# Slot stage of a hard-routed feed-forward: matmul order, a third buffer for turned one-hots, wider loads and stores

## The chip, the cores and the metric

The kernel is one launch on one core of a Trainium2 chip. The metric is the device time of that launch in microseconds. The kernel before took 5747.51 us, the median of three runs (5745.52 to 5748.87).

## The reference

The program computes, on x of shape (16, 256, 128) in float32:

1. causal attention with 16 heads of 8, added to x and normalised;
2. a "fast feed-forward" block: x is standardised to xn; q, k and v each come from a hard-routed feed-forward of xn; attention over 256 tokens; then y + fff(y) with a fourth one, f; added and normalised;
3. a gated causal scan;
4. six layers of local attention (16 heads of 64, window 32) and gated feed-forward; added and normalised.

The change is in part 2. One hard-routed feed-forward (D = 128, LW = 16, DEPTH = 8, 255 nodes, 256 leaves) is

```python
node = zeros
for _ in range(8):
    logit = einsum('bsd,bsd->bs', x, nw[node]) + nb[node]
    node = 2 * node + 1 + (logit > 0)
leaf = node - 255
h = act(einsum('bsd,bsdl->bsl', x, w1[leaf]) + b1[leaf])
out = einsum('bsl,bsld->bsd', h, w2[leaf]) + b2[leaf]
```

so each of the 4096 tokens goes down a tree to a leaf of its own and through that leaf's 128x16 and 16x128 matrices.

## The kernel before

Five engines run in order, each its own stream of instructions, and wait for each other by semaphores: PE (matmul), ACT, DVE, POOL and SP (which issues plain DMAs). routed_feed_forwards (L686) runs twice: for q, k and v together (modules m = 0, 1, 2), and later for f alone. In it:

**Routing.** All node logits of a token are one matmul (L855), the leaf's one-hot comes from a second (L862). Eight leaves form a chunk, so 32 chunks of 128 hidden columns. Counting the tokens by chunk gives each token a position: its chunk's tokens fill whole slots of 128 rows, 64 slots in all (positions, L1110, on DVE). A token's row holds its 128 values and 32 bf16 one-hot values of its leaf within the chunk: ROW = 144 words. POOL writes the rows to DRAM (leaf_rows) with 32 indirect DMAs per module (scatter), and reads the results back from leaf_out with 32 more (gather), in the order scatter 0, 1, 2, gather 0, 1, 2.

**Slots.** Four slots are a group, q; a module has 16 groups. SP loads a group (L812) into one of three xrow buffers, with 128 partitions x 4 pieces of 576 bytes. Then:

- PE turn(q), L889: four fp32 transposes into px (L896) and four bf16 matmuls that turn the one-hots into pl (L898);
- ACT turned(q), L997: copies px to xT (two buffers) and pl to ohT (two buffers). The second copy waits for out_done of group q-2, as that group's output matmuls read the same ohT buffer;
- DVE first_weights(q), L1155: reads each slot's chunk number into a register and copies that chunk's first weights to W1 (L1171) and its bias rows to B_slot (L1173);
- PE hidden(q), L909: per slot, an fp32 matmul (L918, two passes in hardware) and a bf16 matmul that adds bias and a mask of the other leaves (L919); ACT takes the activation to hm (L1010);
- PE second(q), L922: per slot, an fp32 matmul with the second weights (L929, two passes) and a bf16 one for the bias (L930); ACT copies py to yrow (L1016, two buffers); SP stores it to leaf_out (L820).

The order on PE is turn(i), hidden(i-1), second(i-2), then four register loads of chunk numbers for group i (chunks_of); turn(i+1) waits until both copies of turned(i) are done. ACT's order is turned(i), hidden(i-1), outputs(i-2). The last module's routing (m = 2) is laid between the steps i = 0 to 15, a part in each step; k's and f's routing runs ahead of the slots. SP goes through load(i), then store(i-5). The weights of a module are 4 MB, loaded by load_weights in four DMAs; v's take q's place after q's last store.

Of the kernel before, what the change touches and what calls it, by code (L numbers as in the profile page):

```python
# [8 lines left out]
BF16 = mybir.dt.bfloat16  # L9
F32R = mybir.dt.float32r  # L10
U32 = mybir.dt.uint32
# [7 lines left out]
D = 128  # L19
# [567 lines left out]
CHUNKS = 32  # L587
# [8 lines left out]
SRING = 3  # L596

# [88 lines left out]
def routed_feed_forwards(nc, dram, src, modules, act_func, rows_dram, out_dram, scattered, gathered, bias_dram, KV):  # L686
# [6 lines left out]
    with ExitStack() as ctx:  # L693
# [3 lines left out]
        def sb(name, shape, dt=F32):  # L697
# [14 lines left out]
        one_row = sb("one_row", [128, 1])  # L712
        spare = modules[0][1][:].rearrange("p t d -> p (t d)")
        bias_rows = spare[:, 0:512 * n_mod].rearrange("p (m n) -> p m n", n=512)
        bias_rest = spare[:, 512 * n_mod:1024 * n_mod].rearrange("p (m n) -> p m n", n=512)
        late = KV[:].rearrange("p a t d -> p (a t d)")
        nodes = spare[:, 1024 * n_mod:(1024 + LEAVES) * n_mod].rearrange("p (m n) -> p m n", n=LEAVES)
        bias_parts = late[:, 0:n_mod * PIECES * 256].bitcast(BF16).rearrange("p (m c n) -> p m c n", c=PIECES, n=512)
        bits = sb("bits", [128, 2, 2, GT], BF16)
        onehot = sb("onehot", [128, 2, 2, GT], BF16)  # L720
        oc = sb("oc", [128, 2, CHUNKS, NT], BF16)
        mod8 = sb("mod8", [128, 2, NT, BROWS], BF16)
        place = sb("place", [128, CHUNKS, NT])
# [5 lines left out]
        pos_f = sb("pos_f", [128, NT])  # L729
        pos = sb("pos", [128, n_mod, NT], U32)  # L730
# [4 lines left out]
        W = sb("W", [128, CHUNKS, 256])  # L735
# [4 lines left out]
        xrow = sb("xrow", [128, SRING, SG, ROW])  # L740
        xT = sb("xT", [128, 2, SG * 128])
        ohT = sb("ohT", [BROWS, 2, SG * 128], BF16)
        hm = sb("hm", [128, 2, SG * 128])
        yrow = sb("yrow", [128, 2, SG * 128])
# [9 lines left out]
            oc_done oc_ready cnt_done before_ready place_ready count_ready small restart_set tiles_ready chunk_ready pos_ready mod_ready  # L754
# [18 lines left out]
        @block.sync  # L773
        def _(sp):
            for dst, name in consts:
                sp.dma_start(dst[:], dram[name]).then_inc(s["consts_in"], 16)
            for m, (name, _) in enumerate(modules):
                sp.dma_start(nodes[:, m], dram[name + "_nw"]).then_inc(s["nodes_in"], 16)
                sp.dma_start(node_b[:, m], dram[name + "_nb"]).then_inc(s["nodes_in"], 16)
            for m, (name, _) in enumerate(modules):  # L780
                sp.dma_start(bias_rows[:, m, :].rearrange("p (h n) -> p h n", h=2), dram[name + "_b"].rearrange("(h p) n -> p h n", h=2))\
                    .then_inc(s["bias_in"], 16)
            def load_weights(m):

# [20 lines left out]
            def load(q):  # L805
                m, G = divmod(q, SGROUPS)
                r = q % SRING
                if q >= SRING:
                    sp.wait_ge(s["xt_done"], q - SRING + 1)
                if G == 0:  # L810
                    sp.wait_ge(scattered[m], 16 * NT)
                sp.dma_start(xrow[:, r], rows_dram[m % 2][128 * SG * G:128 * SG * (G + 1)].rearrange("(j p) c -> p j c", p=128))\  # L812
                    .then_inc(s[f"in{r}"], 16)

            def store(q):
                m, G = divmod(q, SGROUPS)
                sp.wait_ge(s["y_ready"], q + 1)
                if G == 0 and m >= 2:
                    sp.wait_ge(gathered[m - 2], 16 * NT)
                sp.dma_start(out_dram[m % 2][128 * SG * G:128 * SG * (G + 1)].rearrange("(j p) c -> p j c", p=128),  # L820
                             yrow[:, q % 2].rearrange("p (j c) -> p j c", j=SG)).then_inc(s[f"y_out{q % 2}"], 16)
                if G == SGROUPS - 1 and m + 2 < n_mod:
                    load_weights(m + 2)

            for i in range(n_steps + SRING + 2):
                if i < n_steps:
                    load(i)
                if i >= SRING + 2:
                    store(i - SRING - 2)

        @block.tensor
        def _(pe):
# [56 lines left out]
            def turn(q):  # L889
                r = q % SRING  # L890
                pe.wait_ge(s[f"in{r}"], 16 * (q // SRING + 1))
                if q >= 1:
                    pe.wait_ge(s["xt_ready"], q)
                    pe.wait_ge(s["oh_ready"], q)
                for j in range(SG):
                    nc.tensor.transpose(px[:, 128 * j:128 * j + 128], xrow[:, r, j, 0:D], ident[:])  # L896
                for j in range(SG):
                    mm = nc.tensor.matmul(pl[0:BROWS, 128 * j:128 * j + 128], xrow[:, r, j, D:ROW].bitcast(BF16), ident_b[:],  # L898
                                          start=True, stop=True)
                mm.then_inc(s["xt_done"], 1)  # L900
# [20 lines left out]

            def second(q, chunks):  # L922
# [3 lines left out]
                for j in range(SG):  # L926
                    cols = slice(128 * j, 128 * j + 128)
                    w = weights[q // SGROUPS][:, bass.ds(chunks[j], 1), 128:256].rearrange("p o n -> p (o n)")
                    nc.tensor.matmul(py[:, cols], hm[:, q % 2, cols], w, start=True, stop=False)  # L929
                    mm = nc.tensor.matmul(py[:, cols], ohT[:, q % 2, cols], B_slot[:, q % 3, j, 128:256],  # L930
                                          start=False, stop=True)
# [46 lines left out]
        def _(act):  # L978
# [18 lines left out]
            def turned(q):  # L997
# [14 lines left out]
            def outputs(q):  # L1012
                act.wait_ge(s["out_done"], q + 1)
                if q >= 2:
                    act.wait_ge(s[f"y_out{q % 2}"], 16 * (q // 2))
                nc.scalar.activation(yrow[:, q % 2, :], py[:], ACT.Copy).then_inc(s["y_ready"], 1)  # L1016
# [22 lines left out]
        def _(pool):  # L1039
# [32 lines left out]
            def gather(m):  # L1072
                for half in range(2):
                    pool.wait_ge(s[f"y_out{half}"], 16 * SGROUPS // 2 * (m + 1))
# [14 lines left out]
        def _(dve):  # L1089
# [20 lines left out]
            def positions(m):  # L1110
# [21 lines left out]
                nc.vector.scalar_tensor_tensor(place[:], tiles_at[:].unsqueeze(2).to_broadcast([128, CHUNKS, NT]), 128.0, place[:],  # L1132
                                               ALU.mult, ALU.add).then_inc(s["tiles_ready"], 1)
                dve.wait_ge(s["tiles_ready"], 3 * m + 1)
                nc.vector.tensor_tensor(place[:], place[:], oc[:, m % 2], ALU.mult).then_inc(s["tiles_ready"], 1)
                dve.wait_ge(s["tiles_ready"], 3 * m + 2)
                nc.vector.tensor_reduce(pos_f[:], place[:].rearrange("p c t -> p t c"), AX_X, ALU.add).then_inc(s["tiles_ready"], 1)
                dve.wait_ge(s["tiles_ready"], 3 * m + 3)
                nc.vector.tensor_copy(pos[:, m, :], pos_f[:]).then_inc(s["pos_ready"], 1)
# [357 lines left out]
def layouts_b(i):  # L1497

    out = {}
    for m in "qkvf":  # L1500
# [10 lines left out]
        out[m + "_w"] = w.reshape(CHUNKS, D, 256)  # L1511
# [1186 lines left out]
```

## Time and profile before

| | us |
|---|---|
| median of three runs | 5747.51 |
| profiled execution, whole | 5710.15 |
| its span, first to last instruction | 5708.4 |
| causal attention, up to | 883 |
| q, k, v: routing and slots | 883 to 1606 |
| last gather, attention over tokens | 1606 to 1720 |
| f: routing, scatter, slots, gather | 1720 to 2034 |
| residual, norm, scan | 2034 to 2270 |
| six layers of local attention | 2270 to 5708 |

The profile is of one execution. Times in rows are microseconds from the start of its span. PE is matmul, PEld PE's weight load (it overlaps PE). PEclk is the share of full speed that the clock throttle grants to PE. "[idle before <-releaser]" at the end of a row says how long the engine was idle ahead of it and who ended that. A row with x2 or x4 merges that many instructions.

### The profile page before, as it was taken

Reading aid. Unit: us, or ns where it says so; the run is one execution under the profiler, and the core shown is the slowest. Engines: PE = TensorE matmul, PEld = TensorE weight load, DVE = VectorE, ACT = ScalarE, POOL = GpSimd, SP = SyncE. Lnnn points to the kernel's source line nnn. Section 1 sums busy time; section 2 is a strip of 40 time slices with the busy share of each in tenths; the row PEclk is TensorE's granted clock in tenths of the full one; section 3 lists DMA queues with packets and bytes.
Section 4 is the critical chain, followed back from the end, with each engine's and each line's share of the span. In section 5 each row is a group of like instructions: output and inputs, shape, how many; then the busy total and the mean of one; then the engine's idle time right before and its main releaser. Section 6 shows DMA issues by size and latency. Waiting matters only on the chain. (4 is left out here: it accounts for less than half of the span.)

```text
span 5708.4 us, 191262 instructions
## 1 busy us (share of the span) xinstructions
PE 4628.9 (81%) x74176; PEld 3577.0 (63%) x74192; DVE 3909.8 (68%) x6605; ACT 3409.6 (60%) x6019; POOL 2762.6 (48%) x3241
## 2 busy tenths in 40 slices
PE   7888855659754824799999989998999899989993
PEld 3444422435432513688778877887788788878881
DVE  4666644321123136799889988998899889989983
ACT  3554411112121104689779977997898789878981
POOL 2222203240222011677667766776677577767750
PEclk8888857765566556899999999999999999999995
DMA  2000003132202100211111111111111111121110
GB/s 93 1 0 0 0 0 112 57 94 56 59 25 78 48 11 16 56 47 45 53 51 46 45 49 50 45 46 54 50 45 46 55 44 47 44 59 45 46 41 15
DMA packets 214059, 253.21 MB, mean 44 GB/s; under 512 B 34996, under 2 KB 139700, under 8 KB 211636
## 3 DMA queue, kind: packets, MB, share of 16 engines
q1 hardware_dynamic: 205524, 230.77, 14.4%
q0 software_dynamic: 8192, 17.84, 1.0%
q8 instruction: 218, 3.57, 0.3%
q14 instruction: 125, 1.02, 0.1%
HBM read 70.76 MB, written 39.32 MB: 19 GB/s over the span
## 5 line engine op out<-in xcount | busy, mean ns | idle before, releaser
L2398 POOL TENSOR_TENSOR d_rc<-d_rc,d_rs 128x512 f32<-128x512 f32 x768 | 964.4, 1277 | 537.9 <-DVE d_rs L2481 523.6
L2408 POOL TENSOR_TENSOR d_rc<-d_rc,d_inv 128x1024 f32<-128x1024 f32 x384 | 722.9, 1903 | 161.1 <-DVE d_inv L2502 159.3
L1964 PE MATMUL d_pair<-d_W_high,d_xs_high 128*128 128x512 f32 x1152 | 525.8, 456 | 106.4 <-DVE d_W_low L2467 40.7
L2481 DVE TENSOR_TENSOR d_rc<-d_pair,d_rot 128x512 f32<-128x512 f32 x768 | 528.3, 688 | 102.5 <-ACT d_sq L2213 81.7
L2481 DVE TENSOR_TENSOR d_rs<-d_pair,d_rot 128x512 f32<-128x512 f32 x768 | 523.5, 682 | 0.0
L2213 ACT ACTIVATE d_sq<-d_pair 128x512 f32<-128x512 f32 x768 | 435.9, 597 | 126.8 <-PE d_pair L1964 112.1
L1964 PE MATMUL d_pair<-d_W_high,d_xs_low 128*128 128x512 f32 x1152 | 465.1, 404 | 5.7 <-issue 5.7
L1964 PE MATMUL d_pair<-d_W_low,d_xs_high 128*128 128x512 f32 x1152 | 464.6, 403 | 0.0
L2491 DVE TENSOR_REDUCE d_ss<-d_sq 128x16 f32<-128x1024 f32 x384 | 448.6, 1211 | 0.0
L2111 PE MATMUL d_pair<-d_OT,d_Wo 128*128 128x128 f32 x3072 | 380.4, 278 | 0.0
L2008 PE MATMUL d_pair<-d_ident,d_rc 128*128 128x128 f32 x3072 | 367.6, 273 | 1.0 <-ACT d_sq L2213 1.0
L2111 PEld LDWEIGHTS d_pair<-d_OT,d_Wo 128*128 128x128 f32 x3072 | 364.6, 195 | 0.1
L2008 PEld LDWEIGHTS d_pair<-d_ident,d_rc 128*128 128x128 f32 x3072 | 342.8, 141 | 2.1 <-issue 1.7
L1964 PEld LDWEIGHTS d_pair<-d_W_high,d_xs_high 128*128 128x128 f32 x1152 | 221.3, 192 | 187.3 <-issue 89.3
L2050 PEld LDWEIGHTS d_pair<-d_KT,d_QT 64*32 64x32 f32 x24576 | 256.1, 105 | 129.4 <-issue 129.4
L2083 PE MATMUL d_pair<-d_VW,d_PT 64*32 64x64 f32 x18432 | 300.5, 228 | 44.5 <-issue 44.3
L2509 DVE TENSOR_REDUCE d_mx<-d_pair 128x16 f32<-128x1024 f32 x192 | 234.8, 1223 | 142.5 <-PE d_pair L2050 142.4
L2050 PE MATMUL d_pair<-d_KT,d_QT 64*32 64x64 f32 x24576 | 291.2, 226 | 44.4 <-issue 44.3
L2083 PEld LDWEIGHTS d_pair<-d_VW,d_PT 64*32 64x32 f32 x18432 | 258.4, 106 | 108.6 <-issue 108.6
L2083 PE MATMUL d_pair<-d_V,d_PT 64*32 64x64 f32 x6144 | 300.0, 229 | 14.4 <-issue 14.4
L2262 ACT ACTIVATE d_V<-d_pair 128x512 f32<-128x512 f32 x384 | 227.9, 594 | 139.7 <-PE d_pair L2083 100.4
L312 ACT ACTIVATE a_first<-a_bank,a_late_bias,a_later 128x256 bf16<-128x256 f32 x256 | 128.9, 565 | 282.3 <-PE a_bank L162 282.1
(348 smaller groups left out, 11836.6 us busy)
## 6 DMA issues: line engine op xcount, KB each, us to landing
d_VW<-d_V SPq DMA_DIRECT2D x768, 128.0 KB, 2.4
d_VW<-d_V SPq DMA_DIRECT2D x576, 64.0 KB, 2.0
q_xrow<-leaf_rows SPq DMA_DIRECT2D x48, 288.0 KB
leaf_out<-q_yrow SPq DMA_DIRECT2D x48, 256.0 KB
d_W_whole<-Wqkv_dram SPq DMA_DIRECT2D x7, 1536.0 KB, 7.5
leaf_rows<-a_zeros SPq DMA_DIRECT2D x8, 1152.0 KB, 11.8
f_xrow<-leaf_rows SPq DMA_DIRECT2D x16, 288.0 KB, 3.2
q_W<-q_w_dram SPq DMA_DIRECT2D x4, 1024.0 KB, 10.2
```

The lines of the kernel that those rows point to most:

```text
L1964: mm = nc.tensor.matmul(target, x_part[:, t.par, :], w_part[:, c, :], start=n == 0, stop=n == 2)
L2008: mm = nc.tensor.transpose(ps[:, hp // 4, (hp % 4) * 128:(hp % 4) * 128 + 128], source(hp), ident[:])
L2050: mm = nc.tensor.matmul(s_pair[WIN * w:WIN * w + WIN, odd, hp * DH:hp * DH + DH], QT[rows, hp, WIN * w:WIN * w + WIN], KT[rows, hp, at + W ...
L2083: mm = nc.tensor.matmul(o_pair[WIN * w:WIN * w + WIN, odd, hp * DH:hp * DH + DH], PT[rows, hp, WIN * w:WIN * w + WIN], window_values(t, w, ...
L2111: mm = nc.tensor.matmul(proj_bank[:, 0:128], Wo[:, hp, :], OT[:, hp, :], start=hp == 0, stop=hp == HP - 1)
L2213: nc.scalar.activation(sq[:, half, 512 * j:512 * j + 512], ps[:, j, :], ACT.Square).then_inc(s[f"s{qk}{j}_ready"], 1)
L2262: nc.scalar.activation(V[:, t.par, j, :], v_pair[:, j, :], ACT.Copy).then_inc(s[f"v{j}_ready"], 1)
L2398: nc.gpsimd.tensor_tensor(own[:, :, a, :], own[:, :, a, :], other[:, :, 1 - a, :], ALU.add).then_inc(s[f"add{qk}_ready"], 1)
L2408: nc.gpsimd.tensor_tensor(heads(rc[:, t.par, half, :]), heads(rc[:, t.par, half, :]), inv[:, t.par, half, :].unsqueeze(2).to_broadcast([12 ...
L2481: ins = nc.vector.tensor_tensor(heads(target), heads(ps[:, j, :]), rot[:, t.par, half, cs, :].unsqueeze(1).to_broadcast([128, HP, DH]), AL ...
L2491: nc.vector.tensor_reduce(ss[:, half, :], heads(sq[:, half, :]), AX_X, ALU.add).then_inc(s[f"ss{qk}_ready"], 1)
L2509: nc.vector.tensor_reduce(mx[:], s_pair[:].rearrange("p a (h n) -> p (a h) n", n=DH), AX_X, ALU.max)\
```

## The change

- hidden and second issue the four fp32 matmuls of a group first and the four bf16 ones after them. The whole group is one accumulation: start at its first matmul, stop at its last.
- ohT has three buffers; turned(q) waits for the output matmuls of group q-3.
- SP loads and stores two groups at once (WIDE = 8 slots). In DRAM a block of 1024 rows is now laid out with 8 consecutive rows per partition, so each partition moves one piece. So that a token still comes to its slot, positions gets five integer operations that reorder the bits of a row number.
- The weights in DRAM are laid out by partition first, so a partition's part of a load is one piece. load_weights(0) is issued after the bias parts are stored, since the bias staging now lies in W.
- bits, onehot and place lie in q's output tensor, which makes room; so POOL's first gather waits until the last chunk numbers are made.

```diff
+WIDE = 2 * SG
...
+        place = spare[:, 1024:2048].rearrange("p (c t) -> p c t", t=NT)
+        bits = spare[:, 2048:3072].bitcast(BF16).rearrange("p (b j t) -> p b j t", j=2, t=GT)
+        onehot = spare[:, 3072:4096].bitcast(BF16).rearrange("p (b j t) -> p b j t", j=2, t=GT)
...
-        xrow = sb("xrow", [128, SRING, SG, ROW])
+        xrow = sb("xrow", [128, SRING, WIDE, ROW])
-        ohT = sb("ohT", [BROWS, 2, SG * 128], BF16)
+        ohT = sb("ohT", [BROWS, 3, SG * 128], BF16)
-        yrow = sb("yrow", [128, 2, SG * 128])
+        yrow = sb("yrow", [128, 2, WIDE * 128])
...
-                    sp.dma_start(weights[m][:, chunks, :], dram[name + "_w"][chunks].rearrange("c p n -> p c n")).then_inc(s[f"w_in{m}"], 16)
-            load_weights(0)
+                    sp.dma_start(weights[m][:, chunks, :], dram[name + "_w"][:, chunks, :]).then_inc(s[f"w_in{m}"], 16)
...
             sp.wait_ge(s["bias_out"], 16 * 2 * PIECES * n_mod)
+            load_weights(0)
...
+            def load(k):
+                m, first = divmod(k, SGROUPS // 2)
+                if k >= SRING:
+                    sp.wait_ge(s["xt_done"], 2 * (k - SRING) + 2)
+                if first == 0:
+                    sp.wait_ge(scattered[m], 16 * NT)
+                sp.dma_start(xrow[:, k % SRING], rows_dram[m % 2][128 * WIDE * first:128 * WIDE * (first + 1)].rearrange("(p j) c -> p j c", j=WIDE))\
+                    .then_inc(s[f"in{k % SRING}"], 16)
...
+            for k in range(n_steps // 2 + SRING + 1):
+                if k < n_steps // 2:
+                    load(k)
+                if k >= SRING + 1:
+                    store(k - SRING - 1)
...
-                    nc.tensor.matmul(ph[:, q % 2, cols], W1[:, q % 2, j, :], xT[:, q % 2, cols], start=True, stop=False)
-                    mm = nc.tensor.matmul(ph[:, q % 2, cols], B_slot[:, q % 3, j, 0:128], ohT[:, q % 2, cols], start=False, stop=True)
+                    nc.tensor.matmul(ph[:, q % 2, cols], W1[:, q % 2, j, :], xT[:, q % 2, cols], start=j == 0, stop=False,
+                                     skip_group_check=True)
+                for j in range(SG):
+                    cols = slice(128 * j, 128 * j + 128)
+                    mm = nc.tensor.matmul(ph[:, q % 2, cols], B_slot[:, q % 3, j, 0:128], ohT[:, q % 3, cols], start=False, stop=j == SG - 1,
+                                          skip_group_check=True)
...
-                if q >= 2:
-                    act.wait_ge(s["out_done"], q - 1)
-                nc.scalar.activation(ohT[:, q % 2, :], pl[0:BROWS, :], ACT.Copy).then_inc(s["oh_ready"], 1)
+                if q >= 3:
+                    act.wait_ge(s["out_done"], q - 2)
+                nc.scalar.activation(ohT[:, q % 3, :], pl[0:BROWS, :], ACT.Copy).then_inc(s["oh_ready"], 1)
...
             def gather(m):
+                if m == 0:
+                    pool.wait_ge(s["chunk_ready"], n_mod)
...
-                nc.vector.tensor_copy(pos[:, m, :], pos_f[:]).then_inc(s["pos_ready"], 1)
+                nc.vector.tensor_copy(pos_i[:], pos_f[:]).then_inc(s["row_ready"], 1)
+                dve.wait_ge(s["row_ready"], 5 * m + 1)
+                nc.vector.tensor_scalar(pos_slot[:], pos_i[:], 7, WIDE - 1, ALU.logical_shift_right, ALU.bitwise_and).then_inc(s["row_ready"], 1)
+                nc.vector.tensor_scalar(pos_row[:], pos_i[:], 127, 3, ALU.bitwise_and, ALU.logical_shift_left).then_inc(s["row_ready"], 1)
+                nc.vector.tensor_scalar(pos_i[:], pos_i[:], 0xFFFFFC00, None, ALU.bitwise_and).then_inc(s["row_ready"], 1)
...
+                nc.vector.tensor_tensor(pos_row[:], pos_row[:], pos_slot[:], ALU.bitwise_or).then_inc(s["row_ready"], 1)
...
+                nc.vector.tensor_tensor(pos[:, m, :], pos_row[:], pos_i[:], ALU.bitwise_or).then_inc(s["pos_ready"], 1)
```

second changes as hidden does, store as load does.

## Rows read from the trace of the kernel before

**Rows 1.** The page: granted TensorE clock in 40 slices, in tenths.

```profile
PEclk8888857765566556899999999999999999999995
```

**Rows 2.** Busy time by stage: us, busy (instructions) of PE, PEld, DVE, ACT, POOL; PEclk; DMA share; GB/s.

```profile
1210.00:1286.00 76.00, 13.47 (x47) 8.38 (x46) 2.10 (x8) 2.68 (x6) 50.34 (x53) 0.50 0.34 112
1286.00:1436.00 150.00, 138.31 (x486) 88.49 (x487) 27.15 (x123) 33.13 (x63) 5.67 (x6) 0.50 0.21 59
...
1474.00:1606.00 132.00, 121.15 (x420) 77.34 (x420) 21.23 (x96) 28.33 (x54) 0.00 (x0) 0.50 0.18 49
...
1820.00:1981.00 161.00, 146.44 (x512) 93.53 (x512) 19.63 (x112) 35.77 (x65) 0.00 (x0) 0.50 0.19 53
```

**Rows 3.** Order of time, one step, low clock: start, us, engine, line, instruction, idle before.

```profile
1385.33 1.09 PE L896 MATMUL q_ps_x<-q_ident,q_xrow 128*128 128x128 f32 x4 [0.77 <-ACT q_ohT L1004]
1386.35 0.61 PE L898 MATMUL q_ps_leaf<-q_ident_b,q_xrow 128*32 128x128 bf16 x4
...
1386.89 0.80 PE L918 MATMUL q_ps_hid<-q_xT,q_W 128*128 128x128 f32 x2
...
1387.83 0.80 PE L918 MATMUL q_ps_hid<-q_xT,q_W 128*128 128x128 f32 x2
...
1395.24 1.09 PE L896 MATMUL q_ps_x<-q_ident,q_xrow 128*128 128x128 f32 x4 [0.77 <-ACT q_ohT L1004]
```

**Rows 4.** Waits, 1300 to 1430 us: us in total, times, longest.

```profile
ACT q_ohT L1004 <- PE q_ps_y L930: 90.0, 13, 6.9
```

**Rows 5.** Order of time, steps under routing, high clock.

```profile
1117.01 0.49 PE L918 MATMUL q_ps_hid<-q_xT,q_W 128*128 128x128 f32 x2
...
1117.59 0.49 PE L929 MATMUL q_ps_y<-q_W,q_hm 128*128 x2
...
1120.73 0.63 PE L896 MATMUL q_ps_x<-q_ident,q_xrow 128*128 128x128 f32 x4 [0.77 <-ACT q_ohT L1004]
...
1121.61 0.55 PEld L862 LDWEIGHTS q_ps_route<-q_bits,q_paths 128*128 128x128 bf16 x4
...
1154.87 0.63 PE L896 MATMUL q_ps_x<-q_ident,q_xrow 128*128 128x128 f32 x4 [0.77 <-ACT q_ohT L1004]
```

**Rows 6.** The page's groups: busy, mean ns of one, idle before.

```profile
L2111 PE MATMUL d_pair<-d_OT,d_Wo 128*128 128x128 f32 x3072 | 380.4, 278 | 0.0
```

**Rows 7.** Busy time and clock in short stretches.

```profile
889.00:892.50 3.50, 3.50 (x18) 2.90 (x17) 0.00 (x0) 2.09 (x4) 0.00 (x0) 0.50 0.69 159
892.50:896.00 3.50, 2.59 (x16) 1.77 (x16) 0.00 (x0) 2.47 (x5) 0.00 (x0) 0.95 0.95 298
...
1110.00:1111.00 1.00, 0.25 (x3) 0.28 (x4) 0.17 (x2) 0.98 (x3) 0.00 (x0) 1.00 0.00 0
...
1112.00:1113.00 1.00, 1.00 (x2) 0.48 (x3) 0.39 (x3) 0.55 (x1) 0.00 (x0) 0.50 0.53 161
```

**Rows 8.** Order of time: DVE, positions and first weights.

```profile
937.40 0.18 DVE L1139 CAST q_pos<-q_pos_f 128x32 uint32<-128x32 f32 x1
...
1111.69 0.23 DVE L1171 COPY q_W<-q_W 128x128 f32 x1 [0.52 <-issue]
...
1112.56 0.23 DVE L1171 COPY q_W<-q_W 128x128 f32 x1 [0.52 <-issue]
...
1113.64 0.23 DVE L1171 COPY q_W<-q_W 128x128 f32 x1 [0.73 <-issue]
```

**Rows 9.** f's stage: instructions of f_W, and order of time.

```profile
L1171 DVE COPY f_W<-f_W x64: 226/227/442, 1779.9 to 1960.8; 128x128 f32 x64
...
1741.52 0.34 SPq L801 DMA_DIRECT2D f_B<-leaf_bias_f  x1
...
1815.63 0.96 POOL L1069 DMA_INDIRECT leaf_rows<-f_rows,f_pos  x1 [0.30 <-issue]
...
1980.33 0.60 ACT L1016 ACTIVATE f_yrow<-f_ps_y 128x512 f32<-128x512 f32 x1 [4.12 <-PE f_ps_y L930]
1983.88 0.97 POOL L1076 DMA_INDIRECT b_Q<-leaf_out,f_pos  x1 [167.29 <-DMA leaf_out<-f_yrow]
```

More of the change, by code:

```diff
@@ L729, in routed_feed_forwards @@
         pos_f = sb("pos_f", [128, NT])
+        pos_i = sb("pos_i", [128, NT], U32)
+        pos_row = sb("pos_row", [128, NT], U32)
+        pos_slot = sb("pos_slot", [128, NT], U32)
         pos = sb("pos", [128, n_mod, NT], U32)
@@ L753, in routed_feed_forwards @@
         names = """consts_in nodes_in memset_done rows_done rows_ready bits_done bits_ready match_done onehot_ready
-            oc_done oc_ready cnt_done before_ready place_ready count_ready small restart_set tiles_ready chunk_ready pos_ready mod_ready
+            oc_done oc_ready cnt_done before_ready place_ready count_ready row_ready small restart_set tiles_ready chunk_ready pos_ready mod_ready
             in0 in1 in2 w_in0 w_in1 w_in2 bias_in bias_split bias_out b_in mask_in w1_ready b_ready xt_done xt_ready oh_ready hid_done hm_ready out_done y_ready y_out0 y_out1""".split()
@@ L803, in _ @@
                 load_weights(1)
[L805 to L810, printed above, removed]
-                    sp.wait_ge(scattered[m], 16 * NT)
[L812 to L818, printed above, removed]
+            def load(k):
[3 more added lines that the diff above has]
+                if first == 0:
+                    sp.wait_ge(scattered[m], 16 * NT)
+                sp.dma_start(xrow[:, k % SRING], rows_dram[m % 2][128 * WIDE * first:128 * WIDE * (first + 1)].rearrange("(p j) c -> p j c", j=WIDE))\
+                    .then_inc(s[f"in{k % SRING}"], 16)
@@ L819, in store @@
+            def store(k):
+                m, first = divmod(k, SGROUPS // 2)
+                sp.wait_ge(s["y_ready"], 2 * k + 2)
+                if first == 0 and m >= 2:
                     sp.wait_ge(gathered[m - 2], 16 * NT)
-                sp.dma_start(out_dram[m % 2][128 * SG * G:128 * SG * (G + 1)].rearrange("(j p) c -> p j c", p=128),
-                             yrow[:, q % 2].rearrange("p (j c) -> p j c", j=SG)).then_inc(s[f"y_out{q % 2}"], 16)
-                if G == SGROUPS - 1 and m + 2 < n_mod:
+                sp.dma_start(out_dram[m % 2][128 * WIDE * first:128 * WIDE * (first + 1)].rearrange("(p j) c -> p j c", j=WIDE),
+                             yrow[:, k % 2].rearrange("p (j c) -> p j c", j=WIDE)).then_inc(s[f"y_out{k % 2}"], 16)
+                if first == SGROUPS // 2 - 1 and m + 2 < n_mod:
@@ L823, in store @@
                     load_weights(m + 2)
[L825 to L829, printed above, removed]
+            for k in range(n_steps // 2 + SRING + 1):
[3 more added lines that the diff above has]
+                    store(k - SRING - 1)
         @block.tensor
@@ L889, in turn @@
             def turn(q):
-                r = q % SRING
-                pe.wait_ge(s[f"in{r}"], 16 * (q // SRING + 1))
+                r, at = q // 2 % SRING, SG * (q % 2)
+                pe.wait_ge(s[f"in{r}"], 16 * (q // 2 // SRING + 1))
                 if q >= 1:
@@ L895, in turn @@
                 for j in range(SG):
-                    nc.tensor.transpose(px[:, 128 * j:128 * j + 128], xrow[:, r, j, 0:D], ident[:])
+                    nc.tensor.transpose(px[:, 128 * j:128 * j + 128], xrow[:, r, at + j, 0:D], ident[:])
                 for j in range(SG):
-                    mm = nc.tensor.matmul(pl[0:BROWS, 128 * j:128 * j + 128], xrow[:, r, j, D:ROW].bitcast(BF16), ident_b[:],
+                    mm = nc.tensor.matmul(pl[0:BROWS, 128 * j:128 * j + 128], xrow[:, r, at + j, D:ROW].bitcast(BF16), ident_b[:],
                                           start=True, stop=True)
@@ L928, in second @@
                     w = weights[q // SGROUPS][:, bass.ds(chunks[j], 1), 128:256].rearrange("p o n -> p (o n)")
-                    nc.tensor.matmul(py[:, cols], hm[:, q % 2, cols], w, start=True, stop=False)
-                    mm = nc.tensor.matmul(py[:, cols], ohT[:, q % 2, cols], B_slot[:, q % 3, j, 128:256],
-                                          start=False, stop=True)
+                    nc.tensor.matmul(py[:, cols], hm[:, q % 2, cols], w, start=j == 0, stop=False, skip_group_check=True)
+                for j in range(SG):
+                    cols = slice(128 * j, 128 * j + 128)
+                    mm = nc.tensor.matmul(py[:, cols], ohT[:, q % 3, cols], B_slot[:, q % 3, j, 128:256], start=False, stop=j == SG - 1,
+                                          skip_group_check=True)
                 mm.then_inc(s["out_done"], 1)
@@ L1013, in outputs @@
                 act.wait_ge(s["out_done"], q + 1)
-                if q >= 2:
-                    act.wait_ge(s[f"y_out{q % 2}"], 16 * (q // 2))
-                nc.scalar.activation(yrow[:, q % 2, :], py[:], ACT.Copy).then_inc(s["y_ready"], 1)
+                k, odd = divmod(q, 2)
+                if k >= 2 and odd == 0:
+                    act.wait_ge(s[f"y_out{k % 2}"], 16 * (k // 2))
+                nc.scalar.activation(yrow[:, k % 2, 512 * odd:512 * odd + 512], py[:], ACT.Copy).then_inc(s["y_ready"], 1)
             for k in range(NG):
@@ L1072, in gather @@
             def gather(m):
+                if m == 0:
+                    pool.wait_ge(s["chunk_ready"], n_mod)
                 for half in range(2):
-                    pool.wait_ge(s[f"y_out{half}"], 16 * SGROUPS // 2 * (m + 1))
+                    pool.wait_ge(s[f"y_out{half}"], 16 * SGROUPS // 4 * (m + 1))
                 for t in range(NT):
@@ L1131, in positions @@
                 dve.wait_ge(s["place_ready"], 2 * m + 2)
[L1132 removed]
+                nc.vector.scalar_tensor_tensor(place, tiles_at[:].unsqueeze(2).to_broadcast([128, CHUNKS, NT]), 128.0, place,
                                                ALU.mult, ALU.add).then_inc(s["tiles_ready"], 1)
                 dve.wait_ge(s["tiles_ready"], 3 * m + 1)
[L1135 removed]
+                nc.vector.tensor_tensor(place, place, oc[:, m % 2], ALU.mult).then_inc(s["tiles_ready"], 1)
                 dve.wait_ge(s["tiles_ready"], 3 * m + 2)
[L1137 removed]
+                nc.vector.tensor_reduce(pos_f[:], place.rearrange("p c t -> p t c"), AX_X, ALU.add).then_inc(s["tiles_ready"], 1)
                 dve.wait_ge(s["tiles_ready"], 3 * m + 3)
[L1139 removed]
+                nc.vector.tensor_copy(pos_i[:], pos_f[:]).then_inc(s["row_ready"], 1)
[3 more added lines that the diff above has]
+                nc.vector.tensor_scalar(pos_i[:], pos_i[:], 0xFFFFFC00, None, ALU.bitwise_and).then_inc(s["row_ready"], 1)
+                dve.wait_ge(s["row_ready"], 5 * m + 4)
+                nc.vector.tensor_tensor(pos_row[:], pos_row[:], pos_slot[:], ALU.bitwise_or).then_inc(s["row_ready"], 1)
+                dve.wait_ge(s["row_ready"], 5 * m + 5)
+                nc.vector.tensor_tensor(pos[:, m, :], pos_row[:], pos_i[:], ALU.bitwise_or).then_inc(s["pos_ready"], 1)
                 if m >= 1:
@@ L1510, in layouts_b @@
         w[:, :, 1] = a("w2").reshape(CHUNKS, 128, D)
-        out[m + "_w"] = w.reshape(CHUNKS, D, 256)
+        out[m + "_w"] = w.reshape(CHUNKS, D, 256).transpose(1, 0, 2)
         b = np.zeros((CHUNKS, CHUNK_LEAVES, 2, 128), np.float32)
```

14 lines of the change are left out of this document (6 added, 8 removed).

## The prediction

> **What bounds the kernel now.** I read the summary first, then the busy time by stage, then the waits and the order of instructions inside one step of the slot stage, because that is what the edit touches. The summary shows a TensorE clock at 5 tenths in several of its slices, from the seventh to the sixteenth [rows 1]. [...] Two stretches are of another kind: from 1210 to 1286 us, and from 1436 to 1474, POOL issues its indirect transfers and PE hardly runs (13.47 us of the first 76); what PE's work costs there hardly matters.
>
> I call a group of four slots a step. One step at the low clock takes 9.91 us, first transpose to first transpose (1385.33 to 1395.24) [rows 3]. In it PE turns the rows (1.56 us to the first hidden matmul, 1386.89), does four hidden and four output pairs at 0.94 us (1386.89 to 1387.83), 7.52 us, and then waits: the rest, 9.91 - 1.56 - 7.52 = 0.83 us, is ACT's copy to ohT, which starts after PE's last output matmul and holds PE's next transposes (0.77 us of PE idle on that row). Over 130 us ACT's ohT copy waits 90.0 us for PE, 13 times [rows 4]. DVE waits for PE too. So the bound is PE, plus one stall per step.
>
> **The change part by part.** *The third ohT buffer.* The copy waited for the output matmuls of two steps back, which stand at the end of the current step. With three buffers it waits for those of three steps back, long done, so it runs right after the turning. Gone: 0.83 us a step. What PE waits for next is due earlier: ACT's hidden copy has half a step, and the y copy of the step before is due only before the output matmuls.
>
> *Matmuls apart.* A pair of two fp32 passes and one bf16 matmul takes 0.94 us at the low clock (1386.89 to 1387.83) and 0.57 at the high one (1117.01 to 1117.59) [rows 3, 5]. In an unbroken run of fp32 passes of the same 128x128x128 shape each costs 380.4 us / 3072 = 0.124 us, at a clock that is mostly high [rows 6]. So of 0.57 us some 0.23 are the two passes (the mean holds some low clock), and 0.05 the bf16 matmul, half a pass (at the low clock four leaf matmuls, bf16 too, took 0.54 us with their switch, 1386.35 to 1386.89, and four fp32 transposes 1.02 [rows 3]); about 0.29 is the alternation, one switch there and back. At the low clock the same split is 0.43 + 0.11 + 0.40. Eight pairs a step are now two runs, so six of eight alternations go: 6 x 0.40 = 2.4 us at the low clock, 6 x 0.29 = 1.75 at the high one. Bounds: nothing, if the gap belongs to each fp32 pair whatever follows (then the row of 0.124 us could not be), and 8 x 0.40 = 3.2 us. I take six. [...]
>
> At an unchanged clock a step is then 9.91 - 0.83 - 2.4 = 6.7 us.
>
> *The clock.* This is the largest term, and indirect. At the high clock it fell right after the stall: PE idle at 1110 us (busy 0.25 of 1 us), clock still 1.00, and 0.50 at 1112 [rows 7]; it was back at the high level by 1117, where a pair takes 0.57 us [rows 5], after four route matmuls of 512 columns without a pause. In the plain steps, where a switch gap follows every two passes, it never rises [rows 2]. After the change the switch gaps and the stall, 0.83 + 8 x 0.40 = 4.0 us of a low-clock step, shrink to some 0.8, with no pause over 0.3 us. That is far nearer to the route stretch than to the plain step, so I expect the rise within about two steps, and then it should hold: the stall that preceded each fall is gone. [...]
>
> At the high clock a step is 0.88 (turning, 1120.73 to the next weight load at 1121.61) + 2 x (4 x 0.575 - 3 x 0.29 = 1.43) = 3.74 us on PE [rows 5]. DVE becomes a near tie: four slots at 0.87 us (1111.69 to 1112.56) are 3.5 us [rows 8]. ACT's four copies are shorter (4 x 0.6 us, the copy at 1980.33 [rows 9]). I take 3.85 us; 3.6 and 4.6 are the ends (DVE's slow pace, 1.08 us from 1112.56 to 1113.64, four times and 0.3 for its start).
>
> *Loads and stores in pairs of groups.* Half as many on SP, one run of 4608 or 4096 bytes per partition instead of pieces of 576 or 512. They hide behind PE: three buffers are six groups now, and the load is issued five steps ahead. Only the ends show: POOL's gather began at 1983.88, 3.55 us after the start of the last copy at 1980.33, for the store between them [rows 9]; the first load is alike. A transfer twice as large there costs 0 to 1.5 us at each end; 0.75 x 4 = 3 us.
>
> *Row numbers.* Five more small DVE instructions after the cast of the positions (0.18 us [rows 8]), about 0.2 us each, ahead of the scatter: 1 us for each of q, k, f (v's lie under the slots); bounds 0 and 2 us each. 3 us.
>
> *Edits at nothing.* load_weights(0) moves on SP past the bias stores and delays the bias reads queued behind it. In f the bias reads were issued at 1741.52 and DVE's first W1 copy came at 1779.9 [rows 9]: 38 us of cover. The aliased tiles add one wait, of POOL's first gather for the last chunk numbers, which precede it anyway, since POOL scatters v first. Without that cover the bias reads would cost the weights' transfer ahead of them: 4 MB at the 298 GB/s of 892.5 to 896 us [rows 7] is 14 us, each in q and f.
>
> **The sum,** against the profiled execution (span 5708.4, whole 5710.15 us). Steps under routing (1065 to 1175 us): two took 17.07 us ((1154.87 - 1120.73) / 2 [rows 5]); they lose two stalls (1.6), twelve alternations (3.5) and the low stretch between 1111 and 1115 us (half of 3.4, 1.7), which leaves 10.3; with DVE at 8 x 0.87 = 7.0 us and four routing operations on top I take 10.7: 6.4 pairs of steps x 6.4 us = 41 us. Plain steps of q: (150 + 132) / 9.91 = 28.5, times 6.06 = 172 us, less two climbs of two steps at 6.7 us (2 x 5.7 = 11): 161. f: 161 / 9.91 = 16.2, times 6.06 = 98, less one climb: 93. The stretches under POOL's transfers: 0. Added: 6. Together 41 + 161 + 93 - 6 = 289 us, 5421 for the profiled execution. The median of the runs shown is 37 us above it; that difference I carry unchanged: 5747.5 - 289 = 5458 us.
>
> **The rivals.**
> *The clock stays low in plain steps.* For it: they run at 0.50 throughout now. Against: [rows 7]. Then 44.7 steps x 3.2 = 144, + 41 - 6 = 179 us: 5568. [...]
> *DVE becomes the bound,* at 4.6 us a step: 44.7 x 5.3 = 237, - 17 + 41 - 6 = 255 us: 5493. For it: the slow pace in [rows 8]. Against: that pace is rare.
> *The edit doesn't do what it says:* the gap belongs to the fp32 pair. Then the stall alone goes, and the clock stays: 44.7 x 0.83 + 6.4 x 1.6 - 6 = 41 us: 5706. [...] Against: [rows 6].
> *Slower:* neighbouring tokens of a chunk now lie eight rows apart, and POOL's indirect transfers may slow. They go at 0.96 + 0.30 = 1.26 us [rows 9]; of eight series of 32, seven are on the path, 224 transfers. Above 2.55 us each the gain is used up; at 3.0 us it is 5459 + 224 x 1.74 = 5849. Against: the pace is POOL's own, the bytes are the same, and tokens were scattered over the chunks before.
>
> **How the numbers follow.** Forecast 0.66, clock stays low 0.15, DVE 0.10, no effect of the grouping 0.05, slower 0.03, an even outcome 0.01. The forecast's own range is 5410 to 5510 (step 3.6 to 4.6 us; up to 30 us of luck in how far PE gets under POOL's transfers). The range of 5405 to 5570 takes in the low clock and leaves out 0.15 or so. Measurements of this kernel tell 0.2% (11 us) from no change: faster 0.95, same 0.02, slower 0.03.
>
> **What would show it.** In the profile after: PE's wait for ohT gone; runs of eight fp32 passes with one gap behind; granted clock near 1.0 in f's slot work and its span near 68 us instead of 161; plain steps of 3.7 to 4.1 us; the gaps under POOL's transfers as long as before. A clock of 0.5 there with steps of 6.7 us means the first rival; steps near 5 with PE waiting for DVE's W1 copy the second.

## The result

The changed kernel takes 5494.61 us (median of 4 runs, 5490.34 to 5499.0), the kernel before 5748.19 (4 runs): ratio 0.956, interval 0.954 to 0.958. The gain is 254 us; 290 were forecast (5458). The profiled execution took 5493.6 us, its span is 5491.8.

The granted clock by slices, and the busy time by stage, in the columns of [rows 2]:

```profile
PEclk8877776687687569999999999999999999999995
```
```profile
1110.00:1176.00 66.00, 55.06 (x430) 39.94 (x433) 29.29 (x106) 28.95 (x55) 0.00 (x0) 1.00 0.24 86
...
1300.00:1356.00 56.00, 45.85 (x379) 36.66 (x377) 21.00 (x95) 26.66 (x48) 0.00 (x0) 0.98 0.34 121
1404.00:1452.00 48.00, 39.23 (x316) 31.57 (x315) 17.16 (x78) 22.59 (x40) 0.00 (x0) 0.95 0.25 93
1684.00:1746.00 62.00, 50.73 (x427) 40.57 (x426) 18.29 (x104) 31.31 (x56) 0.00 (x0) 0.99 0.29 100
```
The slot work that stood at 0.50 in [rows 2] now runs at 0.95 to 1.00, and f's slots, from the first turned group to the start of the gather, take 82 us instead of 163. To the start of the last copy of outputs it is 78 us (1678.90 to 1756.86), where 68 were forecast for the stretch that took 161 before. And PE is busy only 82 of 100 us there, where it was busy 92: part of what was saved on PE has become idle time of PE. One step of f, PE alone, then what PE waited for between 1686 and 1742 us (the wait, then us in total, times, longest):

```profile
1704.46 0.63 PE L900 MATMUL f_ps_x<-f_ident,f_xrow 128*128 128x128 f32 x4 [0.99 <-issue]
...
1705.02 0.40 PE L902 MATMUL f_ps_leaf<-f_ident_b,f_xrow 128*32 128x128 bf16 x4
...
1705.35 1.16 PE L922 MATMUL f_ps_hid<-f_xT,f_W 128*128 128x128 f32 x8
...
1706.44 0.39 PE L926 MATMUL f_ps_hid<-f_ohT,f_B_slot 32*128 32x128 bf16 x4
...
1706.76 1.16 PE L937 MATMUL f_ps_y<-f_W,f_hm 128*128 x8
...
1707.85 0.39 PE L940 MATMUL f_ps_y<-f_B_slot,f_ohT 32*128 32x128 bf16 x4
...
1709.13 0.63 PE L900 MATMUL f_ps_x<-f_ident,f_xrow 128*128 128x128 f32 x4 [0.89 <-issue]
```
```profile
PE f_ps_x L900 <- issue: 10.2, 11, 1.0
```
The two blocks of matmuls are as forecast: 1705.35 to 1706.76 is 1.41 us (1.43 in the prediction). The step is not: 4.67 us here, 4.70 on average, against 3.85. The missing 0.85 us is one pause, 0.89 us ahead of the next transposes, and "issue" says that no semaphore held it. What PE's sequencer (it runs ahead of the matmuls: the first read behind them in PE's stream begins at 1706.46, and they end at 1708.24) did in it stands in the view of line L911, the reads of chunk numbers (kind, times, ns, first and last start):

```profile
L911 PEldq TENSOR_LOAD <-f_chunk_no x4: 296/298/305, 1706.5 to 1708.4; - x4
L911 PEldq FUSED_REGOPS  x4: 146/148/151, 1706.8 to 1708.7; - x4
L911 PEldq SEQ_ASSERT  x4: 18/18/18, 1707.0 to 1708.9; - x4
```
Each of the four reads takes 0.64 us to the start of the next. They begin at 1706.46, behind the step's last matmul in the sequencer's order, and end at 1708.96, while the queued matmuls run out at 1708.24 (1707.85 + 0.39). So the stall on ohT of [rows 3] is gone, and a pause of about the same length for the reads stands in its place.

Where the time went, by the starts of the stages in the two traces (us):

| | before | changed | less |
|---|---|---|---|
| attention and norm, unchanged code, up to the first transpose of part 2 | 888.4 | 922.2 | -33.8 |
| q, k, v: routing up to the first turned group | 118.8 | 120.2 | -1.4 |
| first 16 steps (with v's routing between them) | 178.2 | 146.0 | 32.2 |
| the other 32, to the start of the last gather | 424.0 | 277.4 | 146.6 |
| last gather and attention over tokens | 115.5 | 115.8 | -0.3 |
| f: routing up to the first turned group | 96.0 | 97.3 | -1.3 |
| f: slots, to the start of the gather | 163.0 | 82.0 | 81.0 |
| f's gather to the end, unchanged code | 3724.5 | 3730.9 | -6.4 |
| span | 5708.4 | 5491.8 | 216.6 |

The changed part gives 256.8 us. The unchanged attention is 33.8 us longer in this trace, because the profiled execution of before had a higher clock there:

```profile
300.00:500.00 200.00, 172.24 (x1204) 88.70 (x1204) 135.28 (x213) 91.74 (x165) 42.85 (x44) 0.86 0.00 0
```
```profile
300.00:500.00 200.00, 176.01 (x1192) 90.00 (x1191) 121.05 (x190) 91.93 (x164) 44.41 (x44) 0.80 0.00 0
```
The same code ran at a granted clock of 0.86 in the one (the first row, before) and 0.80 in the other. These 33.8 us are most of the 37 by which the profiled execution of before lay below its median.

### The profile page after: what moved, and what is told of

Read it like the earlier page. It is cut to its first block and busy times, and to the rows that moved or that the text cites. A ratio compares the mean times of both kernels' runs of the same rounds, so it can differ in the third digit from the quotient of the medians.

```text
span 5491.8 us, 191188 instructions
## 1 busy us (share of the span) xinstructions
PE 4393.8 (80%) x74176; PEld 3461.5 (63%) x74192; DVE 3912.9 (71%) x6625; ACT 3422.4 (62%) x6019; POOL 2766.2 (50%) x3241
```

## The experiments

They ran on two other chips (e1 to e8 on one, e9 to e11 on the other), on which the kernel before takes 5590 to 5599 us, and each ratio is to the kernel before on the same chip; what differs is told at e5 and e6. Beside each ratio to the kernel before stand two lengths read from the profile as in the table above: q's (first transposes to the start of the last gather) and f's.

| | median us | ratio (95%) | q | f | plain step |
|---|---|---|---|---|---|
| e5 kernel before | 5592.3 | | 472.1 | 163.0 | 9.91 |
| e1 third buffer | 5535.1 | 0.989 (0.985 to 0.994) | 426.1 | 151.6 | 9.11 |
| e2 grouping | 5320.8 | 0.953 (0.949 to 0.956) | 275.1 | 86.2 | 4.66 to 4.94 |
| e7 third buffer, half the grouping | 5317.0 | 0.951 (0.949 to 0.954) | 288.0 | 89.1 | 7.89, then 4.70 |
| e3 third buffer and grouping | 5314.9 | 0.952 (0.948 to 0.955) | 273.9 | 81.6 | 4.70 |
| e6 changed kernel | 5319.4 | 0.950 (0.948 to 0.952) | 278.7 | 81.9 | 4.70 |
| e4 changed kernel, reads spread | 5276.1 | 0.944 (0.940 to 0.947) | 244.7 | 70.5 | 3.74 to 4.78 |
| e11 the same again | 5284.6 | 0.944 (0.942 to 0.946) | 244.9 | 73.2 | 3.74 to 4.63 |
| e8 the same, no bounds at the read | 5285.7 | 0.944 (0.942 to 0.946) | 249.0 | 73.5 | 3.74 to 4.93 |
| e10 e3 with reads spread | 5271.3 | 0.941 (0.940 to 0.943) | 241.3 | 72.0 | 3.74 to 4.76 |
| e9 e2 with reads spread | 5326.2 | 0.951 (0.949 to 0.953) | 282.9 | 88.1 | 5.1 |

**e1: the third buffer alone.**

```diff
-        ohT = sb("ohT", [BROWS, 2, SG * 128], BF16)
+        ohT = sb("ohT", [BROWS, 3, SG * 128], BF16)
...
-                if q >= 2:
-                    act.wait_ge(s["out_done"], q - 1)
+                if q >= 3:
+                    act.wait_ge(s["out_done"], q - 2)
```

> The kernel before with a third ohT buffer and nothing else. Two theories of what it is worth. (A) At the low clock PE's wait is really for ohT, since its four chunk-number reads (4 x 0.64 us on PE's sequencer) finish while the queued matmuls still run: a plain step falls from 9.91 to about 9.1 us, 44.7 steps x 0.8 = 36 us, and the steps at the high clock gain nothing, because there the reads end as late as the copy does: about 5712 us, ratio 0.994. (B) The reads take the stall's place at the low clock too: 5748 us, ratio 1.000. (C) Removing the stall alone lets the clock rise in the plain steps: over 100 us gained, below 5650 us.

5535 us: the plain step is 9.11 us, as (A) has it. The reads are out of the way there because at the low clock (0.50) the queued matmuls last longer: a pair takes 0.94 us, against 0.57 at the high one [rows 3, 5]. In a step of e5, the kernel before, the reads end at 1264.0, 3 us before the transposes that ohT holds:

```profile
L907 PEldq SEQ_ASSERT  x4: 18/18/18, 1262.0 to 1264.0; - x4
...
1266.99 1.09 PE L896 MATMUL q_ps_x<-q_ident,q_xrow 128*128 128x128 f32 x4 [0.77 <-ACT q_ohT L1004]
```
The ratio is 0.989 where (A) had 0.994. What (A) had wrong is the steps under routing: a pair of them takes 13.84 us in e1's trace, not 17.07. Both members lost 0.8 us, and the low stretch that followed each stall went too. The busy time in two steps under routing, and then in plain steps of the same trace (columns of [rows 2]):

```profile
1087.50:1101.30 13.80, 13.80 (x82) 8.84 (x80) 5.53 (x20) 5.35 (x10) 0.00 (x0) 1.00 0.30 83
...
1198.00:1343.00 145.00, 145.00 (x511) 92.88 (x509) 29.88 (x128) 35.56 (x63) 52.04 (x56) 0.50 0.32 87
```
PE is busy all of the time in both, the first at the high clock and the second at the low one for 145 us on end. So PE's busy share does not tell the two levels apart. It also counts the switches between fp32 and bf16: in the plain steps they are 8 x 0.41 = 3.3 of the 9.11 us.

**e2 and e3: grouping alone, and with the third buffer.** The grouping is the diff of hidden and second.

> The kernel before with the fp32 and the bf16 matmuls of a group apart and nothing else; ohT keeps two buffers, loads and stores as before. (A) The grouping carries nearly the whole gain: the switches go, the clock rises in spite of the ohT copy's stall, and at the high clock PE's chunk-number reads would hold the next transposes as long as the copy does: steps of about 4.7 us, 5490 to 5505 us, ratio 0.956. (B) The stall of each step keeps the clock down: steps of 9.91 - 2.4 = 7.5 us, 44.7 x 2.4 + 20 = 127 us gained, about 5620 us, ratio 0.978.

> The kernel before with both: third ohT buffer and grouped matmuls, but loads, stores, row numbers and weights' layout as before. (A) The wide loads and stores are off the path and the five extra DVE operations cost 1 us each: 5490 us, within 6 us of the changed kernel, ratio 0.955. (B) The wide transfers carry part of the gain (fewer and longer pieces leave the DMA engines to others): 5510 us or more.

Both (A). The grouping alone brings the clock up in spite of the stall (from 1200 to 1240 us, in plain steps of q, it is 1.00, with 7.7 us of waits for ohT), and leaves 0 to 6 us to the third buffer (5320.8 against 5314.9 us, with ratios whose intervals overlap). In the steps under routing too e2 keeps the stall on ohT, and the clock stays at the high level; the busy time and the wait from there:

```profile
1060.00:1110.00 50.00, 42.23 (x330) 30.26 (x328) 21.82 (x80) 19.52 (x40) 0.00 (x0) 1.00 0.33 92
```
```profile
PE q_ps_x L896 <- ACT q_ohT L1010: 7.8, 8, 1.0
```
In e3 two steps of q still run at 0.50 (1148 to 1161 us), and show the grouped step at that level:

```profile
1147.68 1.11 PE L896 MATMUL q_ps_x<-q_ident,q_xrow 128*128 128x128 f32 x4
1148.73 0.61 PE L898 MATMUL q_ps_leaf<-q_ident_b,q_xrow 128*32 128x128 bf16 x4
1149.27 2.08 PE L918 MATMUL q_ps_hid<-q_xT,q_W 128*128 128x128 f32 x8
1151.28 0.60 PE L922 MATMUL q_ps_hid<-q_ohT,q_B_slot 32*128 32x128 bf16 x4
1151.81 2.08 PE L933 MATMUL q_ps_y<-b_KV,q_hm 128*128 x8
1153.82 0.60 PE L936 MATMUL q_ps_y<-q_B_slot,q_ohT 32*128 32x128 bf16 x4
1154.35 0.90 PE L896 MATMUL q_ps_x<-q_ident,q_xrow 128*128 128x128 f32 x3
```
This is 6.67 us, against 9.11 with the third buffer alone: 2.44 us, six switches of 0.41, as the prediction had it (2.4 us, and 6.7 for the step). From there the clock takes the step to 4.70 (0.96 from 1161 to 1175 us, 1.00 from 1200 to 1260).

**e4: where the reads stand.** The same four reads of chunk numbers, laid between the blocks of matmuls (shortened from the edit, the comments say where each stands):

```diff
+                chunk_of(i, 0)      # after turn(i)
+                chunk_of(q + 1, 1)  # in hidden, between fp32 and bf16
+                chunk_of(i, 2)      # after hidden
+                chunk_of(q + 2, 3)  # in second, between fp32 and bf16
-                if i < n_steps:
-                    chunks[i] = chunks_of(i)
```

> The changed kernel with PE's four chunk-number reads of a step no longer in a row at its end, but one after the turning, one between the fp32 and the bf16 matmuls of hidden, one after hidden and one between those of second. (A) If these reads (4 x 0.64 us on the sequencer, of which 0.9 to 1.0 us is not covered by queued matmuls) are what holds a step at 4.70 us, the pause of 0.9 us shrinks to a few tenths, and the step to about 3.9 us, where DVE's four slots (4 x 0.87 + 0.4) are next: some 55 steps x 0.8 = 44 us, about 5450 us, ratio to the kernel before 0.948. (B) If DVE or ACT sets the step, nothing moves: 5495 us, ratio 0.956, and PE's idle time stands elsewhere in the step.

(A). A step of f:

```profile
1496.53 0.65 PE L900 MATMUL f_ps_x<-f_ident,f_xrow 128*128 128x128 f32 x4
1497.12 0.40 PE L902 MATMUL f_ps_leaf<-f_ident_b,f_xrow 128*32 128x128 bf16 x4
1497.44 1.16 PE L931 MATMUL f_ps_hid<-f_xT,f_W 128*128 128x128 f32 x8
1498.54 0.39 PE L936 MATMUL f_ps_hid<-f_ohT,f_B_slot 32*128 32x128 bf16 x4
1498.86 1.16 PE L947 MATMUL f_ps_y<-f_W,f_hm 128*128 x8
1499.95 0.39 PE L951 MATMUL f_ps_y<-f_B_slot,f_ohT 32*128 32x128 bf16 x4
1500.27 0.66 PE L900 MATMUL f_ps_x<-f_ident,f_xrow 128*128 128x128 f32 x4
```
3.74 us without a pause: each read now runs while queued matmuls do. DVE's work per slot is unchanged, so DVE did not set the 4.70 us. Between steps of 3.74 us lie others of up to 4.78. No run tests what sets these, but the trace shows where PE pauses in them. In f from 1489 to 1536 us PE is busy 45.91 of 47, and waits only ahead of second's fp32 block, behind the third read. Most reads take PE's sequencer 0.30 us ahead of their check, some up to 0.74, and the longest one (0.742 us, from 1505.53) stands ahead of the longest pause. Busy time, PE's wait, the reads, and that pause:

```profile
1489.00:1536.00 47.00, 45.91 (x391) 36.66 (x388) 16.76 (x96) 27.84 (x50) 0.00 (x0) 1.00 0.33 117
```
```profile
PE f_ps_y L947 <- issue: 1.0, 3, 0.4
```
```profile
L920 PEldq TENSOR_LOAD <-f_chunk_no x48: 294/302/742, 1489.4 to 1535.3; - x48
```
```profile
1506.83 1.16 PE L947 MATMUL f_ps_y<-f_W,f_hm 128*128 x8 [0.41 <-issue]
```
The step of 4.78 us in q has a read of 0.99 us in the same place. Why a read is slow is not shown. In q, from 1170 to 1250 us, DVE waits for PE only 0.8 us of 80 and PE's sequencer waits up to 0.54 us at hidden for DVE's copies, so DVE is close behind.

**e5 and e6: the two kernels themselves on the chip of e1 to e4.**

> The kernel before itself, once more, for a profile on the chip on which the following runs are made: the runs with third buffer and grouping came from a chip on which it took 5590 us instead of 5748. (A) The difference lies where POOL issues its indirect transfers: there PE's steps take 30 to 54 us on the one and 10 us on the other, and the plain steps take 9.9 us on both. (B) It lies everywhere, as a clock or a slower memory would have it.

> The changed kernel itself, for comparison with third buffer plus grouping alone. (A) Wide loads, row numbers and layouts are worth nothing: its q stage and f stage, from first transposes to last gather, are as long as those of third_group within 5 us on the same kind of chip. (B) They are worth 10 us or more one way, most likely where POOL's transfers run, as there are fewer DMA pieces.

e5 is (A): the plain steps are 9.91 us as before. Of the 156 us between the chips 130 lie in q (472.1 against 602.2) and 21 ahead of its first turned group (97.4 against 118.8). The busy time under POOL's transfers, in e5 and in the changed kernel's trace from the first chip:

```profile
1167.00:1248.00 81.00, 74.09 (x261) 47.46 (x260) 22.05 (x69) 18.67 (x35) 61.83 (x63) 0.50 0.53 161
```
```profile
1214.00:1293.00 79.00, 13.81 (x70) 10.27 (x70) 4.17 (x18) 4.88 (x9) 49.72 (x53) 0.54 0.22 69
```
On the first chip PE does 13.81 us of work in 79 us (before the change 13.47 in 76 [rows 2]), where ACT and DVE do still less; here it does 74.09 in 81. What the chips do differently wasn't tested. The difference probably explains that the gain is 254 us on the one and 278 on the other, where more steps are free to get shorter. e6 is (A) too, at its edge: wide transfers, row numbers and layouts cost q 4.8 us (278.7 against e3's 273.9) and f 0.2; the first two steps of q take 5.16 and 10.67 us instead of 4.22 and 7.43.

**e7: only hidden's matmuls apart.**

> The kernel before with the third ohT buffer, and the matmuls apart only in hidden, as before in second. With the third buffer alone a plain step is 9.11 us with PE busy all of it and the clock at 0.50. Three of eight switches gone would make 9.11 - 3 x 0.41 = 7.9 us at the low clock. (A) The clock goes by how much of the time matmuls stream, not by whether PE shows as busy: the share that is switch gaps falls from 3.2 of 9.1 to 2.0 of 7.9 us, still more than in the grouped step at the low clock (0.8 of 6.7), so it stays low in most plain steps: 7.9 us, ratio about 0.975. (B) Any part of the grouping is enough: steps of 5.0 to 5.2 us at the high clock, ratio about 0.956.

The step at the low clock is 7.89 us, as expected, but (A) is wrong: it holds for two or three steps at a time early in q and for one in f, and then the clock rises and stays up (1.00 from 1171 to 1260 us in q, 0.98 from 1520 to 1570 in f). (B) has the ratio nearly (0.951 against 0.956), with steps that are shorter than its 5.0 to 5.2 us. A step at the high clock (PE, from its transposes to the first pair of second; the next transposes start at 1185.4):

```profile
1180.74 0.63 PE L896 MATMUL q_ps_x<-q_ident,q_xrow 128*128 128x128 f32 x4
1181.30 0.40 PE L898 MATMUL q_ps_leaf<-q_ident_b,q_xrow 128*32 128x128 bf16 x4
1181.63 1.16 PE L918 MATMUL q_ps_hid<-q_xT,q_W 128*128 128x128 f32 x8
1182.72 0.39 PE L922 MATMUL q_ps_hid<-q_ohT,q_B_slot 32*128 32x128 bf16 x4
1183.04 0.49 PE L933 MATMUL q_ps_y<-b_KV,q_hm 128*128 x2
1183.46 0.23 PE L934 MATMUL q_ps_y<-q_B_slot,q_ohT 32*128 32x128 bf16 x1
```
In q after 1171 us such steps take 4.66 to 4.83 us, as with all matmuls grouped: second keeps its switches, and the reads, which stand behind them, are hidden by them. So grouping second is worth almost nothing while the reads stand at the end of the step; what it saves on PE comes back as the pause.

**e8: reads without bounds.** `min_val` and `max_val` are left out of the reads on PE and DVE.

> The changed kernel with PE's chunk-number reads spread over the step, and reads without their bounds check on PE and DVE (two register operations fewer each). With the reads spread, a step took 3.74 us (PE never idle) up to 4.3 us, where DVE's four slots came late. (A) A read costs PE's sequencer about 0.4 instead of 0.64 us, and a slot on DVE about 0.65 instead of 0.87 us, so that all steps take 3.74 us: 10 us less than with the reads spread alone, ratio about 0.942. (B) The slower steps come from something else than DVE's reads: as with the reads spread alone, 0.944.

(B), though not for its reason: the check of the bounds moves to the instruction that uses the number. In f from 1489 to 1536 us PE's reads have lost their register operation (0.15 us) and check (0.018), and second's matmul line, which had one register operation a slot (0.06), has two (0.055 to 0.157 us) and the check (0.018). A slot on DVE takes 0.92 us in this trace, against 0.87. And DVE is what the slower steps wait for here: in f from 1489 to 1536 us PE's sequencer waits at hidden, with DVE's copies the last to come, for 0.05 to 0.76 us (ns: shortest, median, longest):

```profile
L928 PEldq EVENT_SEMAPHORE  x11: 51/263/764, 1492.8 to 1532.7; - x11
```

**e9, e10, e11: the third buffer and the wide transfers once the reads are out of the way.**

> Grouped matmuls and PE's chunk-number reads spread over the step, but two ohT buffers, and loads, stores and layouts as before. It asks what the third buffer is worth once the reads don't stand at the end of a step. (A) Copy and reads both end some 1.05 us after the start of a step's last matmul, so that either alone hides the other; with the reads gone the ohT copy holds the next transposes as long as ever: steps of 4.7 us, ratio 0.952 as with the grouping alone. (B) The copy is not on the path at the high clock: steps of 3.8 to 4.0 us, ratio 0.945.

> The same with three ohT buffers: grouping, third buffer and spread reads, but loads, stores, row numbers and layouts as before. (A) Steps of 3.74 to 4.3 us as in the changed kernel with spread reads, ratio 0.944; against two buffers that makes the third one worth 0.8 us a step, 40 us. The wide loads and stores are worth nothing here either. (B) If the wide transfers pay once the steps are short (a load every 3.9 us instead of every 7.8), some steps wait for xrow, and the ratio is 0.948 or more.

> The changed kernel with spread reads once more, beside the two above on the same chip. (A) 0.944 and steps of 3.9 us on average, DVE's four slots being next; equal within 5 us to the one without wide transfers. (B) 0.940 or less, if the wide transfers save more than the 1 us for each of q, k, v and f that the row numbers cost.

e9 is (A): with two buffers the stall on ohT is back, and spreading the reads gives nothing (0.951 against e2's 0.953, on two chips). What PE waited for from 1190 to 1250 us, and one such step:

```profile
PE q_ps_x L896 <- ACT q_ohT L1025: 8.4, 11, 0.8
```
```profile
1545.70 0.63 PE L896 MATMUL f_ps_x<-f_ident,f_xrow 128*128 128x128 f32 x4 [0.77 <-ACT f_ohT L1025]
...
1548.53 1.15 PE L943 MATMUL f_ps_y<-f_W,f_hm 128*128 x8 [0.41 <-issue]
...
1550.84 0.63 PE L896 MATMUL f_ps_x<-f_ident,f_xrow 128*128 128x128 f32 x4 [0.77 <-ACT f_ohT L1025]
```
It even takes 5.14 us, not 4.7: there is a second pause, of 0.41 us, ahead of second's fp32 block, behind a read that took 0.64 us where most take 0.30. Against that, e10 with three buffers is 55 us faster (5326 to 5271). So either of two waits of about 0.9 us hides the other, and only removing both is worth 50 us. e10 is also 13 us below e11, with intervals that overlap at the edge (0.940 to 0.943 and 0.942 to 0.946); the stages agree in sign (q 3.6 us, f 1.3), so the wide transfers and the row numbers that come with them cost a few us or nothing. Both runs are (A) in their steps. e10's 55 us for the third buffer are more than its 40, and e11's medians lie 13 us apart where 5 were allowed. e10 beats both kernels: 0.941 against 0.950 for the changed one.

## Why the prediction was nearly right

*What bounds the kernel, and the grouping:* right, in size too. Six switches of 0.41 us at the low clock (e3), a block of 1.41 us at the high one. The rival by which the gap belongs to each fp32 pair is refuted: one change of type there and back costs 0.41 us (e1 against e3).

*The clock:* right in direction and result. It needed less than the prediction thought: neither the third buffer (e2) nor all of the grouping (e7). The reason given, that a pause brings it down, is only half right. With the pairs alternating the low stretches under routing went with the stall (e1: 1.00 from 1060 to 1120 us). With the matmuls grouped the stall stays there (e2, 7.8 us in 50) and the clock stays at 1.00, as it does in the grouped plain steps with a pause of 0.9 us in each (1.00 from 1686 to 1742 us of the changed kernel). Either change was enough under routing, and no run separates what it is in the alternation that kept the clock low. Transposes did not hold the clock down: in [rows 7] PE ran only L842's (18 of them) from 889 to 892.5 us, at 0.50, and the next 3.5 us stand at 0.95; in the changed kernel's trace it is 0.95 to 1.00 with transposes in every step.

*The third ohT buffer:* here the step "what PE waits for next is due earlier" failed. It went through ACT's and DVE's copies and left out the four reads on PE's own sequencer, so that "no pause over 0.3 us" became one of 0.9. They stood in the trace of before and were never priced (ns of one: shortest, median, longest):

```profile
L907 PEldq TENSOR_LOAD <-q_chunk_no x192: 294/296/489, 1009.8 to 1589.9; - x192
```
They were hidden at the low clock by the queued matmuls, and the term that the prediction itself expected, the higher clock, uncovered them. 0.85 us x (28.5 + 16.2) steps is 38 us, and 1.6 us more on each of 6.4 pairs of steps under routing is 10 (12.3 us a pair against 10.7; with the reads spread, in e4, it is 10.3). Corrected by both, the forecast's 289 us are 241. Measured were 257 in the changed part: the added operations cost 3 us instead of 6, and 13 us more came out of q (11) and f (2), perhaps under POOL's transfers, where the gain was counted as 0. That these two made up for a third of the miss is luck.

*DVE as the bound:* this rival gave 5493 us, 2 us from the result, and is wrong. e4 leaves DVE's work as it is, and the step falls by 0.8 us. Its steps of 4.6 us had a length near the measured one for another cause; a time that fits is no proof of the mechanism it came from. It may be the next bound, together with the slow reads: the steps of e4 average 3.9 us, and in e8 PE's sequencer waits for DVE.

*Loads, stores, row numbers:* off the path, as predicted; 1.4 us and 1.3 us ahead of the first turned groups of q and f, where the prediction's terms (row numbers of q and k with the first load; those of f with its load) add up to 2.75 and 1.75. *POOL's pace:* q's first scatter issues its 32 transfers within 40.6 us and the first gather within 38.7 to 38.9, in the two traces, so the rival that made the kernel slower did not come.

*The median:* the 37 us were carried, rightly: 34 of them lay in the attention and not in the change.

## What to carry to other kernels

When a stall goes, list everything that stands in that stretch on the same engine, its sequencer's register reads too, and price it at the clock that the change brings, since a faster engine covers less: here the reads ended 2.2 us ahead of the last queued matmul's end at the low clock (e5) and 0.7 us behind it at the high one. Two waits of the same length that ended together were worth 0 to 6 us (the buffer, e2 to e3) and nothing (the reads, e2 to e9) singly, about 50 together: test the second one with the first removed. Before comparing two traces, compare their unchanged stages.

## What the runs showed of the hardware

- Reading a chunk number into a register costs PE's sequencer 0.64 us with its bounds check (0.30 + 0.15 + 0.02 and the gaps between; changed kernel). The first of four in a row began 1.8 us before the queued matmuls ran out; spread out, one at a time, most were hidden (e4: PE busy 45.91 of 47 us). In some the first part took up to 0.74 us in f and 0.99 in q instead of 0.30, with PE idle behind them; why is not known.
- Going from fp32 to bf16 matmuls and back costs 0.41 us at the low clock (e1 against e3: 2.44 us for six), and the row of PE counts it as busy (145.00 of 145 us in e1).
- The same attention code took 887 or 888 us up to the first transpose of part 2 in two profiles (before, e7) and 921 to 927 in eleven; in the two that were compared, before and changed, the granted clock was 0.86 and 0.80 from 300 to 500 us.
- Under POOL's indirect transfers PE was at work 18% of the time on one chip (13.47 of 76 us) and 91% on another (74.09 of 81), in the same kernel before; what the chips do differently stays open.
